# Weighted cross attention: the order of VectorE's two halves and of GpSimd's first subtraction

## The chip, the cores and the metric

One NeuronCore of a Trainium2 chip runs the whole program. The metric is the device time of one execution in microseconds (us); the kernel before took 2415.65 us (median of 3 runs).

## The reference

Four transformer layers are applied in turn to 64 sequences of 128 queries with 128 channels; each of the first three attends with 16 heads of 8 channels to a context of 77 keys. The change touches only the second layer (L1), whose attention multiplies the scores by given weights and masks them:

```python
scores = jnp.einsum('bhqd,bhkd->bhqk', q, k) / jnp.sqrt(jnp.float32(d))
scores = scores * attention_weights
scores = jnp.where(attention_mask, -jnp.inf, scores)
p_attn = jax.nn.softmax(scores, axis=-1)
out = jnp.einsum('bhqk,bhkd->bhqd', p_attn, v)
...
x = queries + out
mu = jnp.mean(x, axis=-1, keepdims=True)
var = jnp.mean(jnp.square(x - mu), axis=-1, keepdims=True)
return (x - mu) * jax.lax.rsqrt(var + LN_EPS) * gamma + beta
```

## The kernel before

The program goes through seven phases, A0, F0, A1, A2, F2, A3, F3. A1 is the layer above. Each phase is a software pipeline over the 64 batches (a batch is one sequence), and a step of it is written out by hand for each engine. In step b, each engine works on several batches: b+1 is being weighted and masked, b has its exponentials taken and transposed, b-1 is normalised, b-2 gets its residual, b-3 its layer norm. An engine executes its own list in order and waits on semaphores for the others. Four batches stand in one turn of the hardware loop, and the first and last steps of the phase are written out without a loop.

The 16 x 77 scores of a query stand in two halves of 8 heads (616 numbers each, half 0 and half 1). In A1:

- TensorE (`scores`, L661) writes the scores of b+1 to four PSUM banks; it does so when VectorE's second weighing of batch b has read the banks.
- VectorE (`step_weighted`) does for b+1 and each half: `weigh` (L905: scores in PSUM times the weights `side`, to `p` in `sb_region`), `mask` (L910: -3e38 times the mask is added, from `p` and `sb_mask` to `p`, all of it in SBUF), and `peak_masked` (L918: the maximum of each head, to `sb_max`). Between them stand `variance` (L976), `invert` (L945, waits for TensorE's `back`, L735), `normalise` (L952), `keep_v` (L925), `sums` (L964), `statistics` (L968) and `aggregate` (L972).
- GpSimd (`cross_gpsimd`) subtracts the maximum from each half (`shift`, L1038): half 1 of batch b first, half 0 of batch b+1 later in the same step. Between them stand `root` (L1055), `residual` (L1046) and `centre` (L1059), and behind them the two instructions of `affine` (L1064, L1067).
- ScalarE takes the exponential of each half that was subtracted (L785), and copies keys, queries and transposed probabilities out of PSUM.
- SyncE loads ahead. The weights of b+3 (L582) go into the buffer of b+1 and wait for its second weighing, the mask of b+3 (L587) waits for the second masking of b+1; the residual and context loads stand between them in its queue.

Of the kernel before, what the change touches and what calls it, by code (L numbers as in the profile page):

```python
# [138 lines left out]
def build_layers(nc, a, out):  # L139
# [3 lines left out]
    with ExitStack() as ctx:  # L143
# [358 lines left out]
        def by_head(ap):  # L502
            return ap.rearrange("p (h k) -> p h k", k=C)
# [5 lines left out]
        def half(ap, k):  # L509

            return ap[:, k * HALF_C:(k + 1) * HALF_C]

        def scores_half(k):

            return four[:, 2 * k * 512:(2 * k + 2) * 512].rearrange("p (b n) -> p b n", n=512)[:, :, 0:QC]

        def by_bank(ap):
            return ap.rearrange("p (b n) -> p b n", n=QC)
# [11 lines left out]
        def wait_earlier(eng, ev, ph, b, k, part=0):  # L530

            if (b + -k).exists:
                eng.wait_ge(ev.sem(b + -k), ev.count(ph, b + -k, part))
            elif phase_before(ph) in cross:
                last = Batch(b.pair + PAIRS, b.par) + -k
                eng.wait_ge(ev.sem(last), ev.count(phase_before(ph), last, part))
# [342 lines left out]
        def cross_vector(dve, ph):  # L879
            w = cross[ph]  # L880

            def half_free(b, k):

                if ph == "A0":
                    wait_earlier(dve, quarter_made, ph, b, 2, 2 * k + 1)
                else:
                    wait_earlier(dve, pT_made, ph, b, 2, k)
# [12 lines left out]
            def weigh(b, k):  # L900
                if k == 0:
                    dve.wait_ge(s_made.sem(b), s_made.count(ph, b))
                    dve.wait_ge(weights_loaded.sem(b), weights_loaded.count(ph, b))
                half_free(b, k)
                nc.vector.tensor_tensor(by_bank(half(p_s[b.par], k)), scores_half(k), by_bank(half(side_s[b.par], k)), ALU.mult)\  # L905
                    .then_inc(s_weighted.sem(b), 1)

            def mask(b, k):
                dve.wait_ge(s_weighted.sem(b), s_weighted.count(ph, b, k))
                nc.vector.scalar_tensor_tensor(half(p_s[b.par], k), half(mask_s[b.par], k), MASKED, half(p_s[b.par], k),  # L910
                                               ALU.mult, ALU.add).then_inc(s_masked.sem(b), 1)

            def peak_masked(b, k):
                dve.wait_ge(s_masked.sem(b), s_masked.count(ph, b, k))

                if (b + -1).exists:
                    dve.wait_ge(shifted.sem(b + -1), shifted.count(ph, b + -1, k))
                nc.vector.tensor_reduce(max_s[:, 8 * k:8 * k + 8], by_head(half(p_s[b.par], k)), AX.X, ALU.max).then_inc(max_made.sem(b), 1)  # L918

            def keep_v(b):  # L920
                dve.wait_ge(v_made.sem(b), v_made.count(ph, b))
                wait_earlier(dve, att_made, ph, b, 2, 1)
                dst = v_s[b.par][:].rearrange("p (h v) -> p h v", v=VPAIR // 2)[:, :, 0:DH]
                src = v_bank[0:C, V_COL:V_COL + D].rearrange("p (h v) -> p h v", v=DH)
                nc.vector.tensor_tensor(dst, src, w["bv"][0:C, :].rearrange("p (h v) -> p h v", v=DH), ALU.add).then_inc(v_kept.sem(b), 1)  # L925
# [48 lines left out]
            def variance(b):  # L974
                dve.wait_ge(mv_made.sem(b), mv_made.count(ph, b))
                nc.vector.tensor_scalar(var_s[b.par][:], mv_s[b.par][:, 1:2], LN_EPS, None, ALU.add).then_inc(var_made.sem(b), 1)  # L976

            def step_weighted(b, has):
                if has(1):
                    weigh(b + 1, 0)  # L980
                    weigh(b + 1, 1)
                if has(-3):
                    variance(b + -3)
                if has(1):
                    mask(b + 1, 0)
                if has(-1):
                    invert(b + -1)
                if has(1):
                    peak_masked(b + 1, 0)
                if has(-1):  # L990
                    normalise(b + -1)
                if has(1):
                    keep_v(b + 1)
                if has(-2):
                    sums(b + -2)
                if has(1):
                    mask(b + 1, 1)
                if has(-2):
                    statistics(b + -2)
                if has(1):  # L1000
                    peak_masked(b + 1, 1)
                if has(-2):
                    aggregate(b + -2)
# [23 lines left out]
        def cross_gpsimd(pool, ph):  # L1027
            w = cross[ph]

            def block_keys(b):  # L1030
                pool.wait_ge(k_kept.sem(b), k_kept.count(ph, b))
                wait_earlier(pool, s_made, ph, b, 2)
                nc.gpsimd.tensor_tensor(by_head(kblk_s[b.par]), kT_s[b.par][:].unsqueeze(1).to_broadcast([D, QH, C]),
                                        spread(rowmask[:], C), ALU.mult).then_inc(kblk_made.sem(b), 1)

            def shift(b, k):
                pool.wait_ge(max_made.sem(b), max_made.count(ph, b, k))
                nc.gpsimd.tensor_tensor(by_head(half(p_s[b.par], k)), by_head(half(p_s[b.par], k)), spread(max_s[:, 8 * k:8 * k + 8], C), ALU.subtract)\  # L1038
                    .then_inc(shifted.sem(b), 1)

            def residual(b):
                if ph == "A0" and b.first:
                    pool.wait_ge(rows_loaded, 3 * 16)
                pool.wait_ge(residual_loaded.sem(b), residual_loaded.count(ph, b))
                wait_earlier(pool, sum_made, ph, b, 2)
                nc.gpsimd.tensor_tensor(xb_s[b.par][:], xr_s[b.par][:], w["bo"][:], ALU.add).then_inc(xb_made.sem(b), 1)  # L1046

            def rstd(b):
                pool.wait_ge(mv_made.sem(b), mv_made.count(ph, b))
                nc.gpsimd.tensor_tensor(var_s[b.par][:], mv_s[b.par][:, 1:2], ln_eps[:, 0:1], ALU.add).then_inc(var_made.sem(b), 1)  # L1050
                root(b)

            def root(b):
                pool.wait_ge(var_made.sem(b), var_made.count(ph, b))
                nc.gpsimd.tensor_tensor(rstd_s[b.par][:], var_s[b.par][:], minus_half[:, 0:1], ALU.pow).then_inc(rstd_made.sem(b), 1)  # L1055
                pool.wait_ge(rstd_made.sem(b), rstd_made.count(ph, b))

            def centre(b):
                nc.gpsimd.tensor_scalar(z_s[b.par][:], t_s[b.par][:], mv_s[b.par][:, 0:1], rstd_s[b.par][:, 0:1],  # L1059
                                        ALU.subtract, ALU.mult).then_inc(z_made.sem(b), 1)  # L1060

            def affine(b):
                pool.wait_ge(z_made.sem(b), z_made.count(ph, b))
                nc.gpsimd.tensor_tensor(zg_s[b.par][:], z_s[b.par][:], w["ln_g"][:], ALU.mult).then_inc(zg_made.sem(b), 1)  # L1064
                pool.wait_ge(zg_made.sem(b), zg_made.count(ph, b))
                wait_earlier(pool, y_stored, ph, b, 2)
                nc.gpsimd.tensor_tensor(y_s[b.par][:], zg_s[b.par][:], w["ln_b"][:], ALU.add).then_inc(y_made.sem(b), 1)  # L1067

            def step(b, has):
                weighted = ph == "A1"  # L1070
                if weighted:
                    if has(0):
                        shift(b, 1)
                    if has(-3):
                        root(b + -3)
                    if has(-1):
                        residual(b + -1)
                    if has(-3):
                        centre(b + -3)
                    if has(1):  # L1080
                        shift(b + 1, 0)
                    if has(-3):
                        affine(b + -3)
                else:
                    if has(-3):
                        rstd(b + -3)
                    if has(-1):
                        residual(b + -1)
                    if has(-3):
                        centre(b + -3)  # L1090
                    if has(2):
                        block_keys(b + 2)
                    if has(-3):
                        affine(b + -3)
            drive(pool, NB, step, reach=REACH)

        FT = GB * T
# [1073 lines left out]
```

## Time and profile before

| | |
|---|---|
| median of 3 runs | 2415.65 us (2414.92 to 2417.21) |
| the profiled execution's own time | 2419.09 us |
| its span, first to last instruction | 2417.3 us |
| VectorE busy over the span | 77% |
| GpSimd busy over the span | 65% |
| phase A1, first to last weighing | 510.7 to 897.6 us |

The shares over the whole span mix seven phases with different limits, so that those of A1 have to be read in a window inside it. Durations of neighbouring instructions on one engine overlap by some hundredths of a microsecond; what an instruction costs its queue is the distance from its start to that of the next.

### The profile page before, as it was taken

The numbers are of one execution on the slowest core, as the hardware profiler recorded it, in microseconds if no ns is written. First come the engines' busy times: TensorE is split into PE (matmuls) and PEld (weight loads), VectorE is DVE, ScalarE is ACT, GpSimd is POOL, SyncE is SP. The second block draws the span as 40 slices with busy tenths as digits, with TensorE's granted clock in tenths as the row PEclk, the third lists the DMA queues.
The fourth block names the chain that finished last, engine by engine and source line by source line (L and its number), as shares of the span: only waits on it lengthen the run. The fifth ranks groups of instructions, "written<-read, shape, count | busy, mean of one in ns | idle before, by whom it ended". The sixth has DMA issues, their size and how long they took to land.

```text
span 2417.3 us, 90082 instructions
## 1 busy us (share of the span) xinstructions
PE 2249.4 (93%) x30214; PEld 1876.4 (78%) x30214; DVE 1862.4 (77%) x4063; ACT 1495.6 (62%) x3472; POOL 1567.2 (65%) x2374
## 2 busy tenths in 40 slices
PE   7999999978888888999999989999999999999799
PEld 5777778966666666777778968888888888888688
DVE  4888881159999996777775678899999999998465
ACT  5888885558888886888885524444444444444343
POOL 2666663139999994666667766666666666666333
PEclk9999999979999998999999989999999999999999
DMA  4111112245555542222221223333333333333121
GB/s 131 45 44 44 45 49 66 68 121 166 169 167 168 164 138 49 52 51 51 51 55 55 68 74 92 95 96 96 96 96 96 97 96 97 95 96 95 53 63 54
DMA packets 443731, 211.95 MB, mean 88 GB/s; under 512 B 206704, under 2 KB 434545, under 8 KB 443505
## 3 DMA queue, kind: packets, MB, share of 16 engines
q1 hardware_dynamic: 443632, 210.69, 32.5%
q8 instruction: 55, 0.90, 0.2%
q14 instruction: 44, 0.35, 0.1%
HBM read 113.54 MB, written 29.88 MB: 59 GB/s over the span
## 4 chain that ended last, share of the span: by engine, by line
PE 55%; POOL 16%; issue 12%; SPq 8%; DVE 4%; ACT 3%; DMA 1%; POOLq 0%; DVEq 0%; ACTq 0%
PE bank L1179 6%; PE bank L1453 6%; PE bank L701 5%; PE bank L1540 5%; PE bank L661 5%; PE bank L1193 4%; POOL sb_region L1038 4%; PE bank L721 3%; POOL sb_rstd L1055 3%; PE bank L1493 3%; SPq L1399 3%; SPq L1402 3%; POOL sb_z L1059 3%; PE bank L1479 2%; PE bank L1517 2%
## 5 line engine op out<-in xcount | busy, mean ns | idle before, releaser
L1739 POOL TENSOR_TENSOR sb_pn<-sb_l,sb_r_all 128x512 f32<-128x512 f32 x128 | 134.8, 1053 | 269.7 <-DVE sb_r_all L1670 228.0
L892 DVE TENSOR_REDUCE sb_max<-bank 128x8 f32<-128x616 f32 x256 | 203.3, 794 | 136.6 <-PE bank L675 69.5
L701 PE MATMUL bank<-sb_ident,sb_region 128*77 128x128 f32 x2048 | 274.5, 277 | 33.5 <-ACT sb_pT L798 32.2
L785 ACT ACTIVATE sb_region<-sb_region 128x616 f32<-128x616 f32 x384 | 276.0, 719 | 22.3 <-POOL sb_region L1038 20.8
L798 ACT ACTIVATE sb_pT<-bank 77x1024 f32<-77x1024 f32 x256 | 261.0, 1020 | 41.9 <-PE bank L701 41.8
L701 PEld LDWEIGHTS bank<-sb_ident,sb_region 128*77 128x77 f32 x2048 | 236.7, 152 | 62.1 <-issue 42.5
L897 DVE TENSOR_TENSOR sb_region<-bank,sb_max 128x616 f32<-128x616 f32 x256 | 204.6, 799 | 18.3
L721 PE MATMUL bank<-sb_pT,sb_v 77*32 77x128 f32 x6144 | 208.8, 276 | 2.8 <-ACT sb_pT L798 2.1
L721 PEld LDWEIGHTS bank<-sb_pT,sb_v 77*32 77x32 f32 x6144 | 155.6, 109 | 71.2 <-issue 65.1
L661 PE MATMUL bank<-sb_region,sb_qT 32*128 32x308 f32 x1536 | 158.8, 483 | 54.5 <-ACT sb_region L813 21.8
L1595 ACT ACTIVATE sb_oT<-bank 128x512 f32<-128x512 f32 x128 | 76.5, 598 | 213.9 <-PE bank L1507 213.9
L1648 DVE TENSOR_TENSOR sb_region<-bank,sb_cosT 128x512 f32<-128x512 f32 x256 | 173.7, 679 | 35.5 <-PE bank L1453 34.9
L1038 POOL TENSOR_TENSOR sb_region<-sb_region,sb_max 128x616 f32<-128x616 f32 x128 | 173.1, 1352 | 32.6 <-DVE sb_max L918 32.6
L1228 ACT ACTIVATE sb_fh<-bank,sb_L_xattn_ffb 128x256 f32<-128x256 f32 x256 | 109.3, 473 | 110.9 <-PE bank L1179 110.9
L1730 POOL TENSOR_TENSOR sb_region<-sb_region 128x512 f32<-128x512 f32 x128 | 162.9, 1273 | 21.8 <-PE bank L1479 13.1
L1648 DVE TENSOR_TENSOR sb_region<-bank,sb_sinT 128x512 f32<-128x512 f32 x256 | 174.2, 680 | 0.0
L1731 POOL TENSOR_TENSOR sb_region<-sb_region 128x512 f32<-128x512 f32 x128 | 165.2, 1291 | 0.0
L1611 ACT ACTIVATE sb_l<-sb_l 128x640 f32<-128x640 f32 x128 | 94.4, 738 | 110.5 <-DVE sb_l L1660 110.5
L1059 POOL TENSOR_SCALAR sb_z<-sb_t,sb_mv,sb_rstd 128x128 f32<-128x128 f32 x192 | 153.8, 801 | 0.6
L1055 POOL TENSOR_TENSOR sb_rstd<-sb_var,sb_minus_half 128x1 f32<-128x1 f32 x192 | 140.3, 731 | 13.5 <-DVE sb_var L976 2.2
L1272 DVE TENSOR_TENSOR sb_ft<-bank,sb_fxb 128x256 f32<-128x256 f32 x96 | 40.6, 423 | 136.2 <-PE bank L1193 131.3
L791 ACT ACTIVATE sb_pT<-bank 77x512 f32<-77x512 f32 x256 | 137.9, 590 | 11.2 <-PE bank L687 7.5
(186 smaller groups left out, 6455.9 us busy)
## 6 DMA issues: line engine op xcount, KB each, us to landing
sb_region<-in_side SPq DMA_DIRECT2D x64, 616.0 KB, 3.8
sb_pT<-sb_region SPq DMA_DIRECT2D x512, 64.0 KB, 2.0
sb_kF<-sb_region SPq DMA_DIRECT2D x512, 64.0 KB, 2.1
scratch_after_A<-sb_y SPq DMA_DIRECT2D x256, 64.0 KB, 1.7
sb_fx<-scratch_after_A SPq DMA_DIRECT2D x96, 128.0 KB, 2.1
sb_mask<-in_mask SPq DMA_DIRECT2D x64, 154.0 KB, 2.3
sb_x<-scratch_after_F SPq DMA_DIRECT2D x128, 64.0 KB, 1.9
sb_ctx<-in_ctxT SPq DMA_DIRECT2D x192, 38.5 KB, 1.9
```

The lines of the kernel that those rows point to most:

```text
L661: mm = nc.tensor.matmul(bank[c][:, 0:QC], qT_s[b.par][rows, :], kblk_s[b.par][rows, :], start=True, stop=(ph == "A1"), skip_group_check=(p ...
L701: mm = nc.tensor.transpose(two[0:C, h * T:(h + 1) * T], p_s[b.par][:, head * C:(head + 1) * C], ident[:])
L721: mm = nc.tensor.matmul(att_bank[32 * i:32 * i + 32, k * T:(k + 1) * T], v_s[b.par][:, first:first + 32], pT_s[k][:, h * T:(h + 1) * T], s ...
L785: nc.scalar.activation(half(p_s[b.par], k), half(p_s[b.par], k), ACT.Exp, scale=SCALE[ph]).then_inc(exp_made.sem(b), 1)
L798: nc.scalar.activation(pT_s[k][:], two[0:C, :], ACT.Copy).then_inc(pT_kept.sem(b), 1)
L892: nc.vector.tensor_reduce(dst, by_bank_and_head(scores_half(k)), AX.X, ALU.max).then_inc(max_made.sem(b), 1)
L897: nc.vector.tensor_tensor(by_bank_and_head(by_bank(half(p_s[b.par], k))), by_bank_and_head(scores_half(k)), spread_max(k), ALU.subtract).t ...
L1038: nc.gpsimd.tensor_tensor(by_head(half(p_s[b.par], k)), by_head(half(p_s[b.par], k)), spread(max_s[:, 8 * k:8 * k + 8], C), ALU.subtract)\
L1055: nc.gpsimd.tensor_tensor(rstd_s[b.par][:], var_s[b.par][:], minus_half[:, 0:1], ALU.pow).then_inc(rstd_made.sem(b), 1)
L1059: nc.gpsimd.tensor_scalar(z_s[b.par][:], t_s[b.par][:], mv_s[b.par][:, 0:1], rstd_s[b.par][:, 0:1], ALU.subtract, ALU.mult).then_inc(z_mad ...
L1648: ins = nc.vector.tensor_tensor(part[what][eo].rearrange("p (n t) -> p n t", t=T), src, table[:].unsqueeze(1).to_broadcast([128, BLOCKS, T ...
L1731: nc.gpsimd.tensor_tensor(turned[what][1][:], ropeC[what][1][:], ropeS[what][0][:], ALU.add).then_inc(added.sem(b), 1)
```

## The change

On VectorE the second weighing moves from right behind the first to behind the first half's peak; the second masking moves ahead of `keep_v` and `sums`, and so `statistics` now follows `sums` at once. On GpSimd the subtraction of half 0 moves ahead of `centre`. No instruction is added or removed, and none changes its operands.

```diff
@@ -978,7 +978,6 @@
             def step_weighted(b, has):
                 if has(1):
                     weigh(b + 1, 0)
-                    weigh(b + 1, 1)
                 if has(-3):
                     variance(b + -3)
                 if has(1):
@@ -987,15 +986,14 @@
                     invert(b + -1)
                 if has(1):
                     peak_masked(b + 1, 0)
+                    weigh(b + 1, 1)
                 if has(-1):
                     normalise(b + -1)
                 if has(1):
+                    mask(b + 1, 1)
                     keep_v(b + 1)
                 if has(-2):
                     sums(b + -2)
-                if has(1):
-                    mask(b + 1, 1)
-                if has(-2):
                     statistics(b + -2)
                 if has(1):
                     peak_masked(b + 1, 1)
@@ -1075,10 +1073,10 @@
                         root(b + -3)
                     if has(-1):
                         residual(b + -1)
+                    if has(1):
+                        shift(b + 1, 0)
                     if has(-3):
                         centre(b + -3)
-                    if has(1):
-                        shift(b + 1, 0)
                     if has(-3):
                         affine(b + -3)
                 else:
```

VectorE, in the loop of A1, from the first half's masking to the second half's peak, before the change (REGISTER_ALU rows compute the count that a wait compares with; `sb_region` holds scores, `sb_max` the peaks):

```order
L910 SCALAR_TENSOR_TENSOR sb_region<-sb_mask,sb_region 128x616
L944 REGISTER_ALU
L945 RECIPROCAL sb_rden<-bank 128x16
L917 REGISTER_ALU
L918 TENSOR_REDUCE sb_max<-sb_region 128x8
L952 TENSOR_TENSOR sb_o<-bank,sb_rden 128x128
L925 TENSOR_TENSOR sb_v<-bank,sb_L_xattn_bv 77x16x8
L964 TENSOR_TENSOR sb_t<-bank,sb_xb 128x128
L909 REGISTER_ALU
L910 SCALAR_TENSOR_TENSOR sb_region<-sb_mask,sb_region 128x616
L968 BN_STATS sb_stats<-sb_t 128x6
L917 REGISTER_ALU
```

The same place of the changed kernel, where both L905 weighings no longer stand together ahead of it:

```order
L910 SCALAR_TENSOR_TENSOR sb_region<-sb_mask,sb_region 128x616
L944 REGISTER_ALU
L945 RECIPROCAL sb_rden<-bank 128x16
L917 REGISTER_ALU
L918 TENSOR_REDUCE sb_max<-sb_region 128x8
L905 TENSOR_TENSOR sb_region<-bank,sb_region 128x616
L952 TENSOR_TENSOR sb_o<-bank,sb_rden 128x128
L909 REGISTER_ALU
L910 SCALAR_TENSOR_TENSOR sb_region<-sb_mask,sb_region 128x616
L925 TENSOR_TENSOR sb_v<-bank,sb_L_xattn_bv 77x16x8
L964 TENSOR_TENSOR sb_t<-bank,sb_xb 128x128
L968 BN_STATS sb_stats<-sb_t 128x6
```

The second weighing stands between the first peak and `normalise`, and the second masking is separated from the first peak by that weighing and one short instruction.

GpSimd, in the same loop, one step from the subtraction of half 1 to `affine`, before the change:

```order
L1038 TENSOR_TENSOR sb_region<-sb_region,sb_max 128x616
L1054 REGISTER_ALU
L1055 TENSOR_TENSOR sb_rstd<-sb_var,sb_minus_half 128x1
L1046 TENSOR_TENSOR sb_xb<-sb_xr,sb_L_xattn_bo 128x128
L1059 TENSOR_SCALAR sb_z<-sb_t,sb_mv,sb_rstd 128x128
L1037 REGISTER_ALU
L1038 TENSOR_TENSOR sb_region<-sb_region,sb_max 128x616
L1064 TENSOR_TENSOR sb_zg<-sb_z,sb_L_xattn_ln_g 128x128
```

And in the changed kernel, whose lines are numbered two lower there:

```order
L1036 TENSOR_TENSOR sb_region<-sb_region,sb_max 128x616
L1052 REGISTER_ALU
L1053 TENSOR_TENSOR sb_rstd<-sb_var,sb_minus_half 128x1
L1044 TENSOR_TENSOR sb_xb<-sb_xr,sb_L_xattn_bo 128x128
L1035 REGISTER_ALU
L1036 TENSOR_TENSOR sb_region<-sb_region,sb_max 128x616
L1057 TENSOR_SCALAR sb_z<-sb_t,sb_mv,sb_rstd 128x128
L1062 TENSOR_TENSOR sb_zg<-sb_z,sb_L_xattn_ln_g 128x128
```

The second of the two large subtractions stands one instruction earlier, and `centre` now stands right ahead of the multiplication that uses its result.

## Rows read from the trace of the kernel before

**Rows 1.** Page: the profiled span.

```profile
span 2417.3 us, 90082 instructions
```

**Rows 2.** Window in A1: length, busy us of PE, PEld, DVE, ACT, POOL; clock; DMA.

```profile
640.00:700.00 60.00, 50.39 (x644) 40.42 (x647) 56.28 (x128) 52.33 (x119) 56.89 (x68) 1.00 0.58 167
```

**Rows 3.** Source view of L905: count, duration ns min/median/max, first and last start.

```profile
L905 DVE TENSOR_TENSOR sb_region<-bank,sb_region x128: 765/790/801, 510.7 to 897.6; 128x616 f32<-128x616 f32 x128
```

**Rows 4.** Timeline of VectorE, one loop step: start us, us, instruction, [idle before].

```profile
706.65 1.51 DVE L905 TENSOR_TENSOR sb_region<-bank,sb_region 128x616 f32<-128x616 f32 x2
708.07 0.14 DVE L976 TENSOR_SCALAR sb_var<-sb_mv 128x1 f32<-128x1 f32 x1
708.13 1.11 DVE L910 SCALAR_TENSOR_TENSOR sb_region<-sb_mask,sb_region 128x616 f32<-128x616 uint8 x1
709.16 0.24 DVE L945 RECIPROCAL sb_rden<-bank 128x16 f32<-128x16 f32 x1
709.36 0.80 DVE L918 TENSOR_REDUCE sb_max<-sb_region 128x8 f32<-128x616 f32 x1
710.07 0.28 DVE L952 TENSOR_TENSOR sb_o<-bank,sb_rden 128x128 f32<-128x128 f32 x1
710.27 0.28 DVE L925 TENSOR_TENSOR sb_v<-bank,sb_L_xattn_bv 77x128 f32<-77x128 f32 x1
710.47 0.28 DVE L964 TENSOR_TENSOR sb_t<-bank,sb_xb 128x128 f32<-128x128 f32 x1
710.67 0.79 DVE L910 SCALAR_TENSOR_TENSOR sb_region<-sb_mask,sb_region 128x616 f32<-128x616 uint8 x1
711.38 0.28 DVE L968 BATCH_NORM_STATS2 sb_stats<-sb_t 128x6 f32<-128x128 f32 x1
711.78 0.80 DVE L918 TENSOR_REDUCE sb_max<-sb_region 128x8 f32<-128x616 f32 x1
...
712.81 1.50 DVE L905 TENSOR_TENSOR sb_region<-bank,sb_region 128x616 f32<-128x616 f32 x2 [0.15 <-PE bank L661]
```

**Rows 5.** Timeline of GpSimd, the same step.

```profile
707.37 1.21 POOL L1038 TENSOR_TENSOR sb_region<-sb_region,sb_max 128x616 f32<-128x616 f32 x1
708.55 1.11 POOL L1055 TENSOR_TENSOR sb_rstd<-sb_var,sb_minus_half 128x1 f32<-128x1 f32 x1
709.89 0.45 POOL L1046 TENSOR_TENSOR sb_xb<-sb_xr,sb_L_xattn_bo 128x128 f32<-128x128 f32 x1 [0.23 <-POOL sb_rstd L1055]
710.33 0.80 POOL L1059 TENSOR_SCALAR sb_z<-sb_t,sb_mv,sb_rstd 128x128 f32<-128x128 f32 x1
711.09 1.44 POOL L1038 TENSOR_TENSOR sb_region<-sb_region,sb_max 128x616 f32<-128x616 f32 x1
712.50 0.45 POOL L1064 TENSOR_TENSOR sb_zg<-sb_z,sb_L_xattn_ln_g 128x128 f32<-128x128 f32 x1
713.11 0.46 POOL L1067 TENSOR_TENSOR sb_y<-sb_zg,sb_L_xattn_ln_b 128x128 f32<-128x128 f32 x1 [0.17 <-POOL sb_zg L1064]
713.53 1.21 POOL L1038 TENSOR_TENSOR sb_region<-sb_region,sb_max 128x616 f32<-128x616 f32 x1
```

**Rows 6.** Timeline of VectorE and GpSimd, the phase's first steps.

```profile
512.10 0.79 DVE L910 SCALAR_TENSOR_TENSOR sb_region<-sb_mask,sb_region 128x616 f32<-128x616 uint8 x1
512.92 0.80 DVE L918 TENSOR_REDUCE sb_max<-sb_region 128x8 f32<-128x616 f32 x1
...
513.80 3.07 POOL L1038 TENSOR_TENSOR sb_region<-sb_region,sb_max 128x616 f32<-128x616 f32 x2 [21.32 <-DVE sb_max L918]
```

**Rows 7.** Timeline of ScalarE and TensorE in two neighbouring steps.

```profile
702.31 0.72 ACT L785 ACTIVATE sb_region<-sb_region 128x616 f32<-128x616 f32 x1
...
705.60 0.80 PE L661 MATMUL bank<-sb_region,sb_qT 32*128 32x308 f32 x8 [0.51 <-ACT sb_region L813]
...
708.38 0.38 PE L735 MATMUL bank<-sb_ident,sb_region 128*128 128x128 f32 x2
```

**Rows 8.** Page, DMA issues: KB each, median us from issue to landing.

```profile
sb_region<-in_side SPq DMA_DIRECT2D x64, 616.0 KB, 3.8
```

## What the change will do to the time

> **What bounds the kernel now.** Only A1's step is changed, so I first looked for the engine that sets the pace there. The busy shares of the window come first: of 60 us VectorE is busy for 56.28 and GpSimd for 56.89, ScalarE for 52.33 and TensorE for 50.39, at full clock [rows 2]. Two engines are full, and the others have some slack. The count of weighings gives the step: 128 weighings are 64 steps, the last step's second one starts at 897.6, so that its first starts some 0.7 earlier, and (896.9 - 510.7) / 63 is 6.13 us on average, the fill included [rows 3]. The step that I show takes 6.16, from 706.65 to 712.81 [rows 4]; I count with 6.14.
>
> Then the timelines of the two full engines, side by side. GpSimd's next subtraction of half 1 starts at 713.53, 6.16 after the one at 707.37, and in between its idle notes are only 0.23 and 0.17, both behind its own results [rows 5]. VectorE has 0.15 noted at the step's end [rows 4]. So GpSimd is the tight one, and VectorE is right behind it.
>
> What the reader has to see next is that durations of one instruction differ with what the other engine does. VectorE's second mask takes 0.79, the first 1.11 [rows 4]. The first is issued at 708.13 while GpSimd subtracts half 1 until 708.58, and ends at 709.24, 0.66 after GpSimd's end [rows 4, 5]. GpSimd's subtraction takes 1.21 beside the weighings, but 1.44 when it is issued at 711.09 into the second mask, which ends at 711.46; it ends at 712.53, 1.07 later, so only 0.14 of its 1.21 had been done [rows 4, 5]. `root`, issued at 708.55 under the first mask (end 709.24), ends at 709.66, 0.42 after the mask [rows 4, 5]. Masks (both inputs in SBUF) and GpSimd's instructions do not run together here: the later one waits for the earlier one's end. Weighings (scores in PSUM) do not hold GpSimd up: 706.65 to 708.16 lies over the subtraction of 1.21.
>
> Today this costs VectorE 0.32 a step (1.11 - 0.79) and GpSimd 0.23 at the subtraction. The second mask is issued before the subtraction of half 0 and goes first, unhurt.
>
> **VectorE's new list, start to start.** Costs are distances between starts in [rows 4] unless said otherwise. First weighing to first mask: the mask now needs the weighing just before it; a peak that needs the mask before it starts 0.03 after its end (512.92 against 512.10 + 0.79) [rows 6], so 0.80 + 0.03 = 0.83 with the variance inside. Mask to `invert` 0.71 (as 710.67 to 711.38), `invert` to peak 0.20, peak to second weighing 0.71, weighing to `normalise` 0.71, to the second mask 0.20, to `keep_v` 0.71, to `sums` 0.20, to `statistics` 0.31 (0.28 + 0.03, now exposed), to the second peak 0.40, to the next weighing 1.03. The sum is 6.01. Today's list without its blocked time is 6.16 - 0.32 = 5.84, so the order alone costs VectorE 0.17, out of two dependences that lose their cover. Taken with nothing else, this would still be under 6.14.
>
> **Where masks now meet GpSimd.** I count from the first weighing.
>
> - Half 1's peak starts 1.03 before the weighing and ends at -0.23; GpSimd follows a peak after 0.08 (513.80 against 512.92 + 0.80) [rows 6], so its subtraction runs from -0.15 to 1.06. The first mask, due at 0.83, ends at 1.06 + 0.66 = 1.72 and not at 1.62: 0.10.
> - `root` waits for that mask and ends at 1.72 + 0.42 = 2.14. `residual` follows after 0.23 and takes 0.44 [rows 5]: 2.81. The first peak starts at 1.84 and ends at 2.64, so the subtraction of half 0 may start at 2.72 and starts at 2.81 (2.72 if `root` hands over faster). Today `centre` stands here for 0.76 (710.33 to 711.09) [rows 5].
> - So the subtraction runs from 2.81 to 4.02. The second mask is due at 0.10 + 0.83 + 0.71 + 0.20 + 0.71 + 0.71 + 0.20 = 3.46, inside it. It ends at 4.02 + 0.66 = 4.68 instead of 4.25: 0.43 lost (0.34 from 2.72). This is the new stall, and it falls on an engine that has no slack for it. Today the same pair meets in the other order.
>
> VectorE's step becomes 6.01 + 0.10 + 0.43 = 6.54, or 6.45 with the earlier start. Behind the blocked mask stand `keep_v`, `sums`, `statistics` and the second peak, for which GpSimd waits.
>
> **The same from GpSimd's side.** Subtraction 1.21, rest of the blocked mask 0.66, `root` 0.42, gap and `residual` 0.67, subtraction 1.21, rest of the second mask 0.66: 4.83. Then `centre`. No row shows it under a mask. Bounds: it runs freely (0.76, beside the mask), or it is held until the mask is done and ends 0.80 - 0.14 = 0.66 after it. After it comes the multiplication, which now waits for `centre`'s result as the last addition does for its own (0.17), then 0.61 and 0.42 [rows 5]. Held: 4.83 + 0.66 + 0.17 + 0.61 + 0.42 = 6.69. Free: 4.83 - 0.66 + 0.76 + 1.20 = 6.13. The smaller gaps between the same instructions, of which the rows have no more than two, could take some 0.2 off. I take it as held, since `root` and the subtraction both are, so that the step lies between VectorE's 6.45 and GpSimd's 6.69, and I take 6.50, nearer to the first, because gaps on GpSimd shrink when it is late.
>
> The Trainium skill (page "SBUF — State Buffer", section "Who interferes with whom") says that a VectorE instruction with two SBUF inputs and a GpSimd instruction that reads SBUF exclude each other for the whole instruction, and that issue order decides which one is held. By that rule `centre` is held too, and GpSimd's own sum is 6.69; by the rows alone it could be 6.13, and VectorE's 6.45 to 6.54 would decide. It speaks against this change either way, and the rows of mask, subtraction and `root` agree with it.
>
> **What else moves, at no cost.** TensorE's next scores wait for the second weighing, which moves from 1.5 to 3.3 within the step. ScalarE's exponential of half 1 starts once GpSimd has subtracted, and the scores follow 3.29 later (702.31 to 705.60) [rows 7]: 1.06 + 0.04 + 3.29 = 4.4, over a microsecond behind 3.3. They are done at 5.2, and the next weighing, 0.25 behind them as now (706.40, 706.65), could start at 5.5, before 6.5. `invert` waits for TensorE's `back`, today ended at 708.76, 2.11 after the weighing; TensorE now runs about a microsecond ahead of VectorE, so it is in time for 1.6. If that lead were gone, `invert` would wait for up to 0.7. SyncE's load of the next weights waits for the second weighing and goes 1.8 later, and the residual, context and mask loads behind it go with it; the weights land in 3.8 [rows 8] and are needed two steps on, over 9 us after their issue. Half 0's exponential is ready earlier, which is worth nothing, as ScalarE takes it last.
>
> **The sum.** The first five distances are fill, in which fewer instructions run, and the second mask is already held. 58 steps at 6.50 - 6.14 = 0.36 give 21 us. The profiled execution took 2419.09 with a span of 2417.3 [rows 1], and would become 2440; the median of the runs is 3.4 below it, so 2415.65 + 21 = 2437. The bounds, 6.40 (VectorE's 6.45 less 0.05 for faster handovers) and 6.69, give +15 and +32: the likeliest case's own range is 2430 to 2446.
>
> **The rivals.**
>
> - *The masks win the race* (chance 0.12). If GpSimd came to half 0's subtraction later than 3.46, it would find the mask running and wait, as now, and VectorE would keep its 6.01 + about 0.05. That is 58 x -0.08 = -5 us: 2411. For it: GpSimd bounds today, so it is the late one. Against it: it would have to be 0.65 later than 2.81, and then the first mask is held far longer (each 0.1 by which GpSimd is late there is 0.1 for VectorE), which lets it catch up. It decides at 0.65.
> - *Nothing changes* (0.10). The two orders alternate from step to step, or the holds are shorter than read, and the mean stays within 0.08 of 6.14: 2416. For it: the durations of rows 4 and 5 are of one phase relation out of several.
> - *Worse than all sums* (0.06). VectorE and GpSimd hold each other in turn and `back` comes late as well: 6.9 a step, +44, 2460.
> - The likeliest case has 0.72.
>
> A measurement of this kernel tells about 0.2% (5 us) from no change. The second rival's 2416 is no change, and the first rival's 2411 lies just at that limit, so that I split its 0.12 into 0.08 and 0.04 and give 0.01 of the second to faster: 0.09 faster, 0.13 within it, 0.78 slower. The range of 8 in 10 leaves out the worst case and most of the first rival: 2413 to 2446.
>
> **What would show it.** In the profile of the changed kernel: steps of about 6.5; first masks near 0.9 and second masks near 1.2 instead of 0.79; subtractions of half 0 back at 1.21; `centre` near 1.3; VectorE without waits for TensorE. Second masks at 0.79 with half 0's subtractions over 1.3 would prove the first rival. If VectorE waited for scores or for `back`, my slack of TensorE would be wrong.

## The result: slower by 44 us, and the profile after

The changed kernel takes 2459.43 us (median of 3 runs, 2458.35 to 2460.03) against 2415.65 before: the ratio is 1.0185, interval 1.0167 to 1.0204. It is 22 us above the predicted 2437 and 13 above the range's end. Direction and place were as forecast; half of the size was not.

The page and three windows of the changed kernel (columns as in [rows 2]; the second is a stretch of 3.4 us), then the source view of the weighing:

```profile
span 2457.6 us, 90082 instructions
...
640.00:700.00 60.00, 46.71 (x599) 37.39 (x598) 55.66 (x116) 46.67 (x106) 53.95 (x63) 0.97 0.48 149
733.30:736.70 3.40, 3.40 (x17) 3.40 (x18) 1.86 (x5) 2.40 (x5) 2.28 (x3) 0.50 0.33 97
736.70:801.60 64.90, 50.08 (x666) 39.72 (x665) 61.42 (x127) 51.04 (x116) 59.42 (x68) 1.00 0.50 152
...
L905 DVE TENSOR_TENSOR sb_region<-bank,sb_region x128: 764/782/801, 509.7 to 941.1; 128x616 f32<-128x616 f32 x128
```

The span grew by 40.3, from 2417.3 [rows 1]. The phase's 128 weighings now reach from 509.7 to 941.1, where they reached from 510.7 to 897.6 [rows 3], so that all of it is in A1 (the last weighing now also stands later within its step). TensorE fell from 50.39 busy of 60 to 46.71, ScalarE from 52.33 to 46.67, GpSimd from 56.89 to 53.95, and VectorE from 56.28 to 55.66 [rows 2]: every engine has more idle time than before. That is the first thing to read. When the busiest engines of a stage get less busy and the stage gets longer, look for a loop of waits between them.

Who waits is in the table of waits of the changed kernel, 600 to 850 us (engine, line, waited for: us in total, times, longest):

```profile
ACT sb_region L845 <- PE bank L721: 48.0, 37, 1.6
PE bank L661 <- DVE sb_v L925: 47.5, 37, 1.4
DVE sb_rden L945 <- PE bank L747: 11.3, 36, 1.5
```

TensorE waits 37 times, 1.3 us each, ahead of the scores (L661), and it waits for `keep_v` (L925). This wait did not exist before: there the scores waited for ScalarE, 0.51 [rows 7]. The timelines of VectorE, GpSimd and TensorE over one step of the changed kernel show why:

```profile
740.76 0.76 DVE L905 TENSOR_TENSOR sb_region<-bank,sb_region 128x616 f32<-128x616 f32 x1
741.44 0.14 DVE L976 TENSOR_SCALAR sb_var<-sb_mv 128x1 f32<-128x1 f32 x1
741.56 1.15 DVE L910 SCALAR_TENSOR_TENSOR sb_region<-sb_mask,sb_region 128x616 f32<-128x616 uint8 x1
742.97 0.26 DVE L945 RECIPROCAL sb_rden<-bank 128x16 f32<-128x16 f32 x1 [0.26 <-PE bank L747]
743.14 0.74 DVE L918 TENSOR_REDUCE sb_max<-sb_region 128x8 f32<-128x616 f32 x1
743.80 0.78 DVE L905 TENSOR_TENSOR sb_region<-bank,sb_region 128x616 f32<-128x616 f32 x1
744.50 0.28 DVE L952 TENSOR_TENSOR sb_o<-bank,sb_rden 128x128 f32<-128x128 f32 x1
744.69 1.14 DVE L910 SCALAR_TENSOR_TENSOR sb_region<-sb_mask,sb_region 128x616 f32<-128x616 uint8 x1
745.75 0.28 DVE L925 TENSOR_TENSOR sb_v<-bank,sb_L_xattn_bv 77x128 f32<-77x128 f32 x1
745.95 0.27 DVE L964 TENSOR_TENSOR sb_t<-bank,sb_xb 128x128 f32<-128x128 f32 x1
746.26 0.29 DVE L968 BATCH_NORM_STATS2 sb_stats<-sb_t 128x6 f32<-128x128 f32 x1
746.68 0.80 DVE L918 TENSOR_REDUCE sb_max<-sb_region 128x8 f32<-128x616 f32 x1
...
747.48 0.77 DVE L905 TENSOR_TENSOR sb_region<-bank,sb_region 128x616 f32<-128x616 f32 x1
```

```profile
740.83 1.22 POOL L1036 TENSOR_TENSOR sb_region<-sb_region,sb_max 128x616 f32<-128x616 f32 x1
742.01 1.12 POOL L1053 TENSOR_TENSOR sb_rstd<-sb_var,sb_minus_half 128x1 f32<-128x1 f32 x1
743.35 0.45 POOL L1044 TENSOR_TENSOR sb_xb<-sb_xr,sb_L_xattn_bo 128x128 f32<-128x128 f32 x1 [0.23 <-POOL sb_rstd L1053]
743.96 1.22 POOL L1036 TENSOR_TENSOR sb_region<-sb_region,sb_max 128x616 f32<-128x616 f32 x1 [0.16 <-DVE sb_max L918]
745.16 1.34 POOL L1057 TENSOR_SCALAR sb_z<-sb_t,sb_mv,sb_rstd 128x128 f32<-128x128 f32 x1
746.59 0.45 POOL L1062 TENSOR_TENSOR sb_zg<-sb_z,sb_L_xattn_ln_g 128x128 f32<-128x128 f32 x1
```

```profile
739.55 0.80 PE L661 MATMUL bank<-sb_region,sb_qT 32*128 32x308 f32 x8 [1.41 <-DVE sb_v L925]
740.28 1.08 PE L721 MATMUL bank<-sb_pT,sb_v 77*32 77x128 f32 x32
...
742.33 0.38 PE L735 MATMUL bank<-sb_ident,sb_region 128*128 128x128 f32 x2
742.54 0.39 PE L747 MATMUL bank<-sb_L_xattn_wo,sb_oT 128*128 128x128 f32 x2
...
746.16 0.80 PE L661 MATMUL bank<-sb_region,sb_qT 32*128 32x308 f32 x8 [1.24 <-DVE sb_v L925]
```

The step is 6.72 (740.76 to 747.48). The subtraction of half 0 starts at 743.96 and holds the second mask, issued at 744.69, until 745.83, 0.65 after the subtraction's own end. `keep_v` follows at 745.75, ends at 746.03, and the scores start at 746.16. From them it takes 3.42 until `invert` (742.97 - 739.55 in the step shown). `invert` waits for two things of TensorE, `back` (L735) and the output projection of the batch before (`project_out`, L747), and the second ended last: `back` was over at 742.71, L747 at 742.93. From `invert` the first peak, the late weighing and the held mask lead to the next `keep_v`. The loop closes in 6.61: 3.42 + 0.17 + 0.66 + 0.70 + 0.19 + 1.06 + 0.28 + 0.13. In the next step the scores start 0.23 behind `keep_v` instead of 0.13 (752.65 to 752.88), and the loop is 6.72. The chain that ended last, followed back from 760 to 737 us, goes through TensorE's scores, `attend`, transposes and L747 and VectorE's peak, weighing and `keep_v`; it holds no instruction of GpSimd, whose part in the loop is the hold of the second mask, 0.35 (1.14 - 0.79).

### The profile page after: what moved, and what is told of

Its sections match the earlier page's. It is cut to its first block, busy times and chain, and to the rows that moved or that the text cites. A ratio compares the mean times of both kernels' runs of the same rounds, so it can differ in the third digit from the quotient of the medians.

```text
span 2457.6 us, 90082 instructions
## 1 busy us (share of the span) xinstructions
PE 2255.2 (92%) x30214; PEld 1884.4 (77%) x30214; DVE 1895.9 (77%) x4063; ACT 1494.6 (61%) x3472; POOL 1585.2 (64%) x2374
## 4 chain that ended last, share of the span: by engine, by line
PE 65%; issue 12%; DVE 8%; POOL 7%; SPq 5%; ACT 2%; DMA 1%; DVEq 0%; POOLq 0%; ACTq 0%
PE bank L701 7%; PE bank L1451 6%; PE bank L661 6%; PE bank L1177 6%; PE bank L721 6%; PE bank L1538 5%; PE bank L1191 4%; PE bank L1491 4%; PE bank L1477 2%; PE bank L1515 2%; DVE sb_region L905 2%; PE bank L1505 2%; SPq L1400 2%; SPq L1397 2%; PE bank L743 1%
## 5 line engine op out<-in xcount | busy, mean ns | idle before, releaser
L661 PE MATMUL bank<-sb_region,sb_qT 32*128 32x308 f32 x1536 | 158.4, 482 | 105.4 <-DVE sb_v L925 81.6
L1036 POOL TENSOR_TENSOR sb_region<-sb_region,sb_max 128x616 f32<-128x616 f32 x128 | 155.6, 1215 | 50.1 <-DVE sb_max L918 48.5
L1057 POOL TENSOR_SCALAR sb_z<-sb_t,sb_mv,sb_rstd 128x128 f32<-128x128 f32 x192 | 185.8, 968 | 0.6
L661 PEld LDWEIGHTS bank<-sb_region,sb_qT 32*128 32x128 f32 x1536 | 63.1, 188 | 149.0 <-issue 138.3
L845 ACT ACTIVATE sb_region<-bank 128x256 f32<-128x256 f32 x192 | 73.6, 383 | 157.7 <-PE bank L721 157.7
```

What stands on the lines that cost most here:

```text
L661: mm = nc.tensor.matmul(bank[c][:, 0:QC], qT_s[b.par][rows, :], kblk_s[b.par][rows, :], start=True, stop=(ph == "A1"), skip_group_check=(p ...
```

## The experiments

Twelve kernels were run, each against the kernel before on the same chip. The last column is the distance from the first step's weighing to the last step's in its trace, divided by 63, fill and all.

| kernel | us | ratio to before (95%) | us a step |
|---|---|---|---|
| before | 2415.65 | | 6.13 |
| changed | 2459.43 | 1.0185 (1.0167 to 1.0204) | 6.80 |
| e1, keep_v ahead | 2439.05 | 1.0103 (1.0087 to 1.0120) | 6.49 |
| e2, VectorE's part alone | 2519.37 | 1.0428 (1.0411 to 1.0446) | 7.76 |
| e3, GpSimd's part alone | 2435.87 | 1.0084 (1.0067 to 1.0101) | 6.49 |
| e4, e1 with GpSimd as before | 2449.28 | 1.0145 (1.0128 to 1.0162) | 6.65 |
| e5, mask ahead of keep_v, alone | 2436.96 | 1.0086 (1.0069 to 1.0103) | 6.42 |
| e6, mask ahead of sums, alone | 2445.39 | 1.0126 (1.0107 to 1.0145) | 6.60 |
| e7, wait at the last bank | 2442.97 | 1.0119 (1.0100 to 1.0137) | 6.56 |
| e8, late weighing alone | 2451.31 | 1.0152 (1.0134 to 1.0170) | 6.70 |
| e9, before, product in PSUM | 2389.72 | 0.9898 (0.9881 to 0.9914) | 5.78 |
| e10, changed, product in PSUM | 2428.08 | 1.0057 (1.0041 to 1.0074) | 6.37 |
| e11, e1, product in PSUM | 2420.75 | 1.0028 (1.0018 to 1.0038) | 6.24 |
| e12, e9, mask early | 2391.32 | 0.9903 (0.9886 to 0.9919) | 5.80 |

Two theories stood after the result. V: the wait of TensorE's scores for `keep_v` closes a loop that the change made longer than a step. H, the prediction's own: the exclusion of masks and GpSimd alone sets the step.

**e1_v_ahead.** The changed kernel, and:

```diff
                 if has(1):
-                    mask(b + 1, 1)
                     keep_v(b + 1)
+                    mask(b + 1, 1)
```

> The changed kernel, with keep_v moved back ahead of the second masking; GpSimd as changed. Theory V (a loop through TensorE: keep_v, scores, attend, back, invert, peak, weighing, masking, keep_v sets the step of 6.72 us, because the next scores wait for keep_v, which the change put behind the second masking): the loop loses the held masking (about 1.1 us) and falls under the holds between VectorE and GpSimd, whose own sum from the changed kernel's trace is 6.50 to 6.56 a step; 2415.65 + 58 x 0.39 is about 2438, and the 1.3 us waits of TensorE before the scores are gone. Theory H (the holds between masks and GpSimd alone set the step; keep_v's place is without weight): 2459, as the changed kernel, since every mask and subtraction stands where it stood.

2439.05, 20.4 us under the changed kernel: V. The waits of TensorE for L925 are gone, and GpSimd runs without a wait for VectorE. Its timeline, from one subtraction of half 1 to the next:

```profile
741.11 1.22 POOL L1036 TENSOR_TENSOR sb_region<-sb_region,sb_max 128x616 f32<-128x616 f32 x1
742.28 1.12 POOL L1053 TENSOR_TENSOR sb_rstd<-sb_var,sb_minus_half 128x1 f32<-128x1 f32 x1
743.62 0.45 POOL L1044 TENSOR_TENSOR sb_xb<-sb_xr,sb_L_xattn_bo 128x128 f32<-128x128 f32 x1 [0.23 <-POOL sb_rstd L1053]
744.04 1.21 POOL L1036 TENSOR_TENSOR sb_region<-sb_region,sb_max 128x616 f32<-128x616 f32 x1
745.24 1.34 POOL L1057 TENSOR_SCALAR sb_z<-sb_t,sb_mv,sb_rstd 128x128 f32<-128x128 f32 x1
746.66 0.46 POOL L1062 TENSOR_TENSOR sb_zg<-sb_z,sb_L_xattn_ln_g 128x128 f32<-128x128 f32 x1
747.28 0.46 POOL L1065 TENSOR_TENSOR sb_y<-sb_zg,sb_L_xattn_ln_b 128x128 f32<-128x128 f32 x1 [0.17 <-POOL sb_zg L1062]
747.70 1.21 POOL L1036 TENSOR_TENSOR sb_region<-sb_region,sb_max 128x616 f32<-128x616 f32 x1
```

That is 6.59, with `root` at 1.12 and `centre` at 1.34, both held by a mask: the prediction's sum from GpSimd's side, at 6.69. Steps with smaller gaps are 6.46, as 747.70 to 754.16.

**e7_wait_at_last_bank.** The changed kernel, and in `scores`, A1 only:

```diff
-                if (b + -1).exists:
+                if ph != "A1" and (b + -1).exists:
                     pe.wait_ge(v_kept.sem(b + -1), v_kept.count(ph, b + -1))
...
-                for c in range(NQ):
+                for c in (0, 2, 3, 1) if ph == "A1" else range(NQ):
+                    if ph == "A1" and c == 1 and (b + -1).exists:
+                        pe.wait_ge(v_kept.sem(b + -1), v_kept.count(ph, b + -1))
```

> The changed kernel, in which TensorE writes the score banks of A1 in the order 0, 2, 3, 1 and waits for keep_v only ahead of bank 1, the one that it shares with the value projection; VectorE and GpSimd as changed. Theory V: the loop scores, attend, back, invert, peak, weighing, held mask, keep_v of 6.72 us loses the three banks' matmuls, about 0.5 us, and GpSimd's own 6.53 is next: 2438 to 2442, as with keep_v moved. Theory H (keep_v's place mattered through VectorE's own order, not through TensorE's wait): 2459.

2442.97, 16.5 us under the changed kernel with VectorE's and GpSimd's lists untouched. Of the wait for `keep_v`, 47.5 us between 600 and 850, no more than 3.3 are left, in 19 weight loads. It is TensorE's wait that cost, not `keep_v`'s place in VectorE's own list. The new order of the banks was not run without the moved wait.

**e2_vector_only.** The changed kernel with `centre` back ahead of `shift(b + 1, 0)`.

> VectorE's list as changed, GpSimd's as before (centre ahead of the subtraction of half 0). Theory V: the loop through keep_v is 6.37 us a step even if no mask is held (3.43 from scores to invert, then 0.17, 0.65, 0.71, 0.20, 0.71, 0.28, 0.22), so still slower than before: 6.37 to 6.5, 2429 to 2437. Theory H (the early subtraction, which holds the second mask, is what costs): the second mask is due about when centre ends and goes first, nothing is held on VectorE, and the time is that of before or under it, 2405 to 2416.

2519.37: 60 us above the changed kernel and 82 above V's upper number. Both theories missed it. VectorE, GpSimd and TensorE in its trace, from 744 us:

```profile
744.85 1.84 DVE L910 SCALAR_TENSOR_TENSOR sb_region<-sb_mask,sb_region 128x616 f32<-128x616 uint8 x1
...
744.83 1.22 POOL L1036 TENSOR_TENSOR sb_region<-sb_region,sb_max 128x616 f32<-128x616 f32 x1
...
747.13 1.01 PE L661 MATMUL bank<-sb_region,sb_qT 32*128 32x308 f32 x8 [2.01 <-DVE sb_v L925]
748.07 1.93 PE L721 MATMUL bank<-sb_pT,sb_v 77*32 77x128 f32 x32
749.93 0.48 PE L743 MATMUL bank<-sb_ident,sb_o 128*128 128x128 f32 x1
750.20 1.92 PE L701 MATMUL bank<-sb_ident,sb_region 128*77 128x128 f32 x8
```

`centre` puts the subtraction right on the second mask: 744.83 against 744.85. The mask is held for 1.05 (1.84 instead of 0.79), `keep_v` comes at 746.62 and the scores at 747.13, after 2.01 of waiting, and then TensorE's matmuls take nearly twice as long (`attend` 1.93, against 1.08 at 740.28 in the changed kernel). The granted clock of 640 to 700 us is 0.84 of full speed in this trace. So the trace shows the loop through `keep_v`, a longer hold in it, and TensorE at its lower level (1.2 GHz instead of 2.4) on top; the parts were not separated.

**e3_gpsimd_only.** The kernel before with `shift(b + 1, 0)` ahead of `centre`.

> VectorE's list as before, GpSimd's as changed. Theory H: the subtraction of half 0 is now issued ahead of the second mask (710.33 against 710.67 in the trace of before) and holds it until 0.66 after its end, 0.74 us more on VectorE, 6.6 to 6.7 a step, 2443 to 2448; the loop through keep_v is untouched here, so this is the price of the holds alone. Theory V alone (GpSimd's order is a detail): keep_v stands ahead of the masking, the loop through TensorE keeps its length, and the time is within 5 us of 2416.

2435.87, about 21 us slower: H is right for this half of the change, at the GpSimd sum again (6.59 and 6.53 in its trace, as e1) and 7 to 12 us under my number. The second mask takes 1.50 as expected, but VectorE's list has more slack than I gave it: from the second peak to the next weighing it needs 0.81 here (747.42 to 748.23), where [rows 4] have 1.03. e3 and e1 cost the same, in which the mask is due at different times: the sum is GpSimd's, which waits for both masks in either order.

**e4_v_ahead_old_gpsimd.** e1 with GpSimd's order as before.

> VectorE's list as changed but with keep_v ahead of the second masking, GpSimd's as before: only the second weighing is late. The loop through keep_v is 5.7 us, no bound for either theory. By the holds the second mask is due 3.66 us after the first weighing and the subtraction of half 0 at 3.57, a race: if the mask goes first, GpSimd's sum is about 6.5 and the time 2437; if the subtraction goes first, the mask is held by about 1 us and the step is near 7.1, 2470. Theory V alone expects the time of before, 2416, or under it.

2449.28. The race is real, and both orders occur within one turn of the loop: in three steps of four the mask goes first (0.78) and the subtraction is held (1.94 to 1.95), in the fourth it is the other way round (1.64 and 1.21). V alone is refuted. In the steps in which the mask goes first, it is recorded after the subtraction:

```profile
710.66 1.95 POOL L1036 TENSOR_TENSOR sb_region<-sb_region,sb_max 128x616 f32<-128x616 f32 x1
710.75 0.78 DVE L910 SCALAR_TENSOR_TENSOR sb_region<-sb_mask,sb_region 128x616 f32<-128x616 uint8 x1
```

**e8_late_weighing_only.** The kernel before with only `weigh(b + 1, 1)` moved behind `peak_masked(b + 1, 0)`.

> The kernel before, with only the second weighing moved behind the first peak. keep_v stays ahead of the second masking, so the loop through it is no bound. Holds: the second mask comes 0.7 later than now against the same GpSimd order, the subtraction of half 0 goes first in some steps and holds it by up to 1 us, in others the mask goes first: 6.5 to 6.7 a step, 2437 to 2449. A theory in which only the early subtraction and the late keep_v cost anything expects 2416.

2451.31, just above the range: the subtraction wins in every step (masks of 1.60 and 1.45), not in some. The masks also hold the first multiplication of `affine` (1.02 instead of 0.46). The late weighing alone costs 35 us.

**e5_mask_ahead_of_v** and **e6_mask_ahead_of_sums.** The kernel before, with the second masking moved ahead of `keep_v` and `sums` (e5), or only of `sums`, as this diff of e6 shows:

```diff
                 if has(1):
                     keep_v(b + 1)
+                    mask(b + 1, 1)
                 if has(-2):
                     sums(b + -2)
-                if has(1):
-                    mask(b + 1, 1)
-                if has(-2):
                     statistics(b + -2)
```

> The kernel before, with the second masking moved ahead of keep_v and sums (statistics then follows sums); both weighings together and GpSimd's order as before. Theory V: the loop through keep_v has neither the weighing nor a held mask in it and is 3.43 + 0.17 + 0.65 + 0.20 + 0.71 + 0.28 + 0.22 = 5.66 us, under 6.14, so a late keep_v by itself costs nothing: 2416 from this side. If a late keep_v cost 20 us wherever it stands, it would be 2436. Holds: the mask would be issued at 710.27, 0.06 ahead of centre (710.33), which would be held for about 0.6 while the subtraction behind it goes free (0.23 less): GpSimd's step 6.15 + 0.35 = 6.5, also 2436, but then with centre at 1.3 us and no wait of TensorE for keep_v, which tells the two apart.

> The kernel before, with the second masking only one place earlier, between keep_v and sums. Theory of holds: in the trace of before centre runs beside a mask that is issued 0.34 us behind it, and then the subtraction is held by the rest of the mask. The mask is now issued 0.14 behind centre and is over when the subtraction comes: GpSimd saves up to 0.2 a step and VectorE bounds at about 6.0 to 6.05, 2408 to 2412, the first version faster than both. If GpSimd arrives so that centre comes just behind the mask, it is held for 0.5 and the step is near 6.5, 2436. If holds are no matter of a tenth of a microsecond, 2416.

e5 takes 2436.96, by a held `centre` (1.41) and without a wait for `keep_v`, so that a late `keep_v` makes nobody wait where the loop through it is short. e6, which I hoped to be faster than before, takes 2445.39. VectorE and GpSimd of e6:

```profile
743.91 0.79 DVE L910 SCALAR_TENSOR_TENSOR sb_region<-sb_mask,sb_region 128x616 f32<-128x616 uint8 x1
...
743.78 1.60 POOL L1057 TENSOR_SCALAR sb_z<-sb_t,sb_mv,sb_rstd 128x128 f32<-128x128 f32 x1
```

The mask is recorded 0.13 behind `centre` and `centre` is held all the same, to 0.68 after the mask's end; in 13 steps it is recorded 0.29 behind and `centre` is held too (1.58, as 703.80 against 704.09). Before, the mask came 0.34 behind it and neither was held (0.80 and 0.79) [rows 4, 5]. The kernel before stands in a narrow good place: one place earlier, some 0.2 us, costs 30 us.

**e9, e10 and e11.** If the two inputs in SBUF make masks and GpSimd exclude each other, it should end when one of them is in PSUM. `weigh` leaves its product in the score banks, `mask` reads it there, and TensorE's next scores wait for the second masking. The same edit on the kernel before (e9), the changed one (e10) and e1 (e11):

```diff
-            taken = s_weighted if ph == "A1" else shifted
+            taken = s_masked if ph == "A1" else shifted
...
-                half_free(b, k)
-                nc.vector.tensor_tensor(by_bank(half(p_s[b.par], k)), scores_half(k), by_bank(half(side_s[b.par], k)), ALU.mult)\
+                nc.vector.tensor_tensor(scores_half(k), scores_half(k), by_bank(half(side_s[b.par], k)), ALU.mult)\
...
-                nc.vector.scalar_tensor_tensor(half(p_s[b.par], k), half(mask_s[b.par], k), MASKED, half(p_s[b.par], k),
+                half_free(b, k)
+                nc.vector.scalar_tensor_tensor(by_bank(half(p_s[b.par], k)), by_bank(half(mask_s[b.par], k)), MASKED, scores_half(k),
```

> The kernel before, in which weigh leaves the product in the score banks and mask reads it there, so that the mask has one input in SBUF and one in PSUM; TensorE's next scores then wait for the second masking. Theory of holds by inputs (a mask and GpSimd exclude each other because the mask reads two tensors in SBUF): no mask and no GpSimd instruction is held any more, masks 0.79, root 0.56, subtractions 1.21; GpSimd's step falls to 5.3 to 5.4, VectorE's to 5.84, TensorE with ScalarE stand at about 5.9, and with 5.9 to 6.0 a step the time is 2402 to 2408, faster than both. If any mask and GpSimd exclude each other whatever the inputs: holds as now, 2416, or slower where the scores wait for the mask.

> The changed kernel with the same edit (product in the score banks, mask reads it there). Holds by inputs: no holds; what is left of the change is its order, the loop scores, back, invert, peak, weighing, masking, keep_v of 3.43 + 0.17 + 0.65 + 0.71 + 0.20 + 0.71 + 0.28 + 0.22 = 6.37 a step: 2429, still slower than before, and this is the price of keep_v's place without any hold. If the holds are not of the inputs: 2459.

> The changed kernel with keep_v ahead of the second masking and with the product in the score banks. Neither a hold nor keep_v in the loop, but the next scores now wait for the second masking, which stands behind the late weighing: 3.43 + 0.17 + 0.65 + 0.71 + 0.20 + 0.20 + 0.79 + 0.22 is again 6.37, 2429, near the run above, since the wait for keep_v is replaced by one for the mask. If only keep_v's place and the holds counted, VectorE's 6.0 would bound: 2408.

e9 takes 2389.72, faster than both. A mask and GpSimd in its trace:

```profile
745.38 0.78 DVE L910 SCALAR_TENSOR_TENSOR sb_region<-sb_mask,bank 128x616 f32<-128x616 uint8 x1
...
745.54 0.56 POOL L1055 TENSOR_TENSOR sb_rstd<-sb_var,sb_minus_half 128x1 f32<-128x1 f32 x1 [0.30 <-DVE sb_var L976]
746.63 0.80 POOL L1059 TENSOR_SCALAR sb_z<-sb_t,sb_mv,sb_rstd 128x128 f32<-128x128 f32 x1
747.40 1.22 POOL L1038 TENSOR_TENSOR sb_region<-sb_region,sb_max 128x616 f32<-128x616 f32 x1
```

`root` runs in 0.56 inside the mask's time, and the mask takes 0.78; `centre` and the subtraction take 0.80 and 1.22. By the Trainium skill (page "SBUF — State Buffer", section "Who interferes with whom") a VectorE instruction with at most one SBUF input, outside the 2-port modes, does not contend with GpSimd; this trace agrees. I had expected 12 to 18 us more than what came, since I kept ScalarE and TensorE at 5.9.

e10 takes 2428.08 (expected 2429). No instruction is held, and its steps are 6.29 to 6.40. The wait for `keep_v` is there:

```profile
742.52 0.28 DVE L925 TENSOR_TENSOR sb_v<-bank,sb_L_xattn_bv 77x128 f32<-77x128 f32 x1
...
743.04 0.80 PE L661 MATMUL bank<-sb_region,sb_qT 32*128 32x308 f32 x8 [1.02 <-DVE sb_v L925]
```

So among the kernels without holds the changed order costs 38.4 us (e10 against e9), and the holds, with the slow stretches of TensorE that come with them (below), cost 31.4 on top of it (2459.43 - 2428.08). e11 takes 2420.75 where I expected 2429: behind a mask the scores start after 0.06, not after the 0.22 that I took from `keep_v`. It also tells how to read the 38.4. With `keep_v` ahead again only 7.3 of them come back, because in e9 to e11 the scores wait for the second mask as well, a wait that this edit brings and the changed kernel does not have. So the 38.4 is the price of the whole order in the edited kernels, and no split of the changed kernel's 44.

**e12_product_in_psum_mask_early.** e9 with `mask(b + 1, 1)` right behind `peak_masked(b + 1, 0)`.

> The kernel before with the product in the score banks (2389.7), and now the second masking right behind the first peak, ahead of normalise, keep_v and sums. With no holds the place of a mask is judged by loops alone. The next scores wait for this masking and for keep_v: 3.43 + 0.17 + 0.65 + 0.71 + 0.20 + 0.28 + 0.22 = 5.66 by keep_v, against 5.75 a step measured with the mask behind sums; VectorE pays 0.11 for statistics right behind sums. 5.66 to 5.75 a step, 2384 to 2390. If a hold is still about, the mask ahead of centre would cost as it did without the edit (20 us or more): 2410.

2391.32, interval as that of e9, where the same kind of move cost e5 and e6 over 20 us: in this kernel the place of a mask has no price of its own once it holds nobody. No gain either; `e9` stands as the best version.

## Why the prediction was wrong in its size

- **What bounds the kernel now**: right in the main. GpSimd and VectorE were full, and taking the holds away (e9) makes the same order 26 us faster. But one step was read for all: from 600 to 850 us VectorE's first weighing waited for the scores in 24 of 41 steps, 8.1 us in total, so that TensorE was closer to the limit than the 0.15 of the step shown.
- **The holds read from durations**: right where it counted. `centre`, which no row showed issued under a mask, is held (1.34). But the general sentence, that a mask and a GpSimd instruction do not run together, was contradicted by the prediction's own rows: `centre` (710.33 to 711.13) and the second mask (from 710.67) overlap by 0.46 with neither longer [rows 4, 5]. The rule that it cites, exclusion for the whole instruction by the order of issue, therefore does not fit the recorded spans to the letter, and in e6 and e4 the order of the recorded starts does not decide who is held. GpSimd's sum of 6.69 was measured as 6.59 and 6.46 to 6.53 in e1, e3 and e7, and VectorE's held second mask as 1.14 (predicted 0.79 + 0.43 or 0.34). The 6.50 that I took is near e1's 6.49, and e1's 2439 near my 2437. (By the prediction's own +32 the upper end is 2448, not 2446.)
- **The step that failed**: "What else moves, at no cost". I wrote there that TensorE's next scores wait for the second weighing, and showed that this has a microsecond to spare; the description of the kernel before names no other wait on VectorE either. In the code the same scores also wait for `v_kept` of the batch before, since the value projection shares bank 1 with them. The change puts `keep_v` behind the late weighing and the held mask, and that wait ended last: 47.5 us in 37 steps. I had listed `keep_v` only as an instruction that is queued behind the mask, and asked who waits for it only of GpSimd. The loop is 6.61 to 6.72 a step instead of 6.50; e1 takes 20.4 us back and e7 16.5. Missing in the same place is `invert`'s wait for L747: the prediction and the description of the kernel name only `back`, which in the changed kernel had ended 0.22 earlier.
- **TensorE's clock**: not thought of. With 1.3 us of waiting in each step the granted clock was 0.50, the lower level of 1.2 GHz, in five stretches of 3.4 us from 535 to 873 (the windows above show one); in each of them the step is 1.2 to 1.7 longer than 6.72, 6.8 us together by the distances between first weighings. Before, A1 had 1.00 in the window [rows 2], as e1 has, and e10 with waits of 1.0. That the waiting brought the clock down is likely from this but was not tested by itself.
- **The account**: the distance from first to last step grew by 42.0. The first five grew by 4.2 (543.69 - 509.74 against 540.38 - 510.68), a slow stretch among them; the other 58 by 37.8, of which some 5.1 are the four other slow stretches and 32.7, 0.56 a step, the loop.
- **The rivals**: "worse than all sums" named 6.9 a step and 2460, near the measured time, and with TensorE coming late for `invert` it had a part of it: `invert` waits 0.3 a step (11.3 us in 36), though for L747 and not for `back`. But it had no wait of the scores in it, so that its 2460 beside the measured 2459 is luck. "The masks win the race" does occur, in e4, and is not faster, because GpSimd is then held for longer.
- **VectorE's new list**: 6.01 by its sum, of which the distances of the changed kernel's trace leave 5.67 (0.80, 0.71 for the unheld mask, 0.17, 0.66, 0.70, 0.19, 0.71, 0.20, 0.31, 0.42 and 0.80). I had 1.03 for the end, where 0.80 is needed. So even with its holds VectorE is not what decides; my 6.45 to 6.54 agreed with GpSimd's sum by luck.

## What to carry to other kernels

Before calling a moved instruction free, list every semaphore wait in the other engines' code that its result feeds, those that only guard a shared PSUM bank too, and close the loop of each one through the moved place; a loop longer than the step sets the new step, and the sign is that all engines get less busy. Where VectorE and GpSimd are both full, read whether durations of the same instruction differ, and ask first whether one of VectorE's two inputs can stay in PSUM: here that was worth 26 us, and none of the orders tried was faster than the one before. A tuned order may sit in a gap of a tenth or two of a microsecond, as this one did, so single moves should be judged by the other engine's timeline at that very moment.

## What the runs showed of the hardware

- When a mask and a GpSimd instruction start close together, the order of the recorded starts does not tell who is held: `centre` started 0.13 and 0.29 ahead of a mask and was held (1.60 and 1.58, e6), 0.34 ahead and was not (0.80, before), while the large subtraction started 0.02 ahead and held the mask to 1.84 (e2), and 0.09 ahead and was itself held to 1.95 (e4). What in the instructions makes the difference was not looked into.
- GpSimd's `root` on one column takes 0.56 alone and 1.12 under a mask; a mask with one input in PSUM takes 0.78 to 0.80 and leaves `root` at 0.56, the one with both in SBUF takes 0.79 when it is not held.
- With TensorE waiting for 1.3 us of each 6.7 its clock stood at the lower level five times, 3.4 us each, in a phase of 430 us; with waits of 2.0 us (e2) the mean of 640 to 700 us was 0.84.
